# A transformer block with a mixture of experts: in SyncE's order, the loads of k directly behind their store

## The reference

```python
mod = (_silu(L0_c) @ L0_wmod).reshape(B, 6, 1, -1)            # sa, ca, ga, sb, cb, gb
h = _layernorm(x) * (1 + ca) + sa
x = x + ga * attention(h)                                      # 16 heads of 16 features, softmax
h = _layernorm(x) * (1 + cb) + sb
x = x + gb * experts(h)
# experts: 2 shared and 16 routed, 256 -> 128 -> 256 with gelu;
# probs = softmax(h @ router.T); the top 4 of 16 are kept as gates, the others are 0
# act = gelu(up_r) * gate;  routed = sum over experts of act @ down
```

## Time and profile before

| | |
|---|---|
| median of 3 runs | 997.27 us (994.63 to 997.33) |
| the profiled execution | 992.75 us, span 991.0 us |
| TensorE busy (matmuls) | 875.2 us, 88% |
| VectorE busy | 673.8 us, 68% |
| ScalarE busy | 614.9 us, 62% |
| GpSimd busy | 387.3 us, 39% |
| DMA, mean rate | 79 GB/s |
| granted TensorE clock, mean over the span | 0.951 |

### The profile page before, as it was taken

The page is one execution under the profiler, slowest core; times in us unless marked ns, Lnnn a source line. Parts: engine busy times, 40 slices in busy tenths (PEclk is TensorE's granted clock), DMA queues, the critical chain, the costliest instruction groups (busy, mean ns, idle before and its releaser), DMA issues.

```text
span 991.0 us, 15808 instructions
## 1 busy us (share of the span) xinstructions
PE 875.2 (88%) x5928; PEld 424.8 (43%) x5928; DVE 673.8 (68%) x1315; ACT 614.9 (62%) x1033; POOL 387.3 (39%) x325
## 2 busy tenths in 40 slices
PE   5478876889989898999989998999989998998897
PEld 3222123224544454444544454444544454455564
DVE  6686676467678777678678777777767778834332
ACT  3246444575767576876777576767578667773443
POOL 4423023122442534344433444344425233454445
PEclk9758789799999999999999999999999999999999
DMA  6804600371032611371133411271135310320230
GB/s 242 171 0 97 107 1 11 55 167 59 2 93 75 140 48 54 55 177 70 44 55 135 76 48 64 46 197 49 55 54 129 97 44 1 115 96 18 81 118 22
DMA packets 50413, 78.37 MB, mean 79 GB/s; under 512 B 8216, under 2 KB 44568, under 8 KB 46240
## 3 DMA queue, kind: packets, MB, share of 16 engines
q1 hardware_dynamic: 50336, 77.36, 29.9%
HBM read 64.31 MB, written 12.89 MB: 78 GB/s over the span
## 4 chain that ended last, share of the span: by engine, by line
PE 48%; DVE 15%; DMA 11%; ACT 10%; issue 6%; POOL 5%; SPq 4%; POOLq 0%; ACTq 0%; DVEq 0%
PE down_bank L889 13%; PE scalar_bank L758 11%; DMA k_aug<-k_parts 8%; PE vector_bank L821 7%; PE vector_bank L803 6%; PE vector_bank L758 4%; PE scalar_bank L803 4%; DVE q_aug L720 4%; DVE gelu L702 3%; ACT f_ring L535 3%; DVE neg_max L715 3%; POOL z_lo L475 3%; ACT probs L558 3%; DVE rows L600 3%; SPq L408 2%
## 5 line engine op out<-in xcount | busy, mean ns | idle before, releaser
L715 DVE TENSOR_REDUCE neg_max<-vector_bank 128x1 f16<-128x512 f32 x512 | 325.5, 686 | 105.6 <-PE vector_bank L803 104.3
L558 ACT ACTIVATE probs<-scalar_bank 128x512 f32<-128x512 f32 x512 | 277.0, 600 | 188.4 <-PE scalar_bank L803 178.7
L517 POOL TENSOR_TENSOR act_lo<-gelu,act_hi 128x512 f16<-128x512 f32 x144 | 185.7, 1312 | 171.9 <-ACT act_hi L549 162.4
L702 DVE TENSOR_TENSOR gelu<-gelu,gates 128x512 f32<-128x512 f32 x128 | 117.3, 929 | 86.5 <-ACT gelu L583 85.9
L803 PE MATMUL vector_bank<-k_aug,q_aug 64*128 64x512 f16 x512 | 130.1, 414 | 44.5 <-DMA k_aug<-k_parts 28.9
L889 PE MATMUL down_bank<-down_hi,act_hi 128*128 128x256 f16 x576 | 159.1, 276 | 2.1 <-POOL act_lo L517 1.7
L889 PE MATMUL down_bank<-down_hi,act_lo 128*128 128x256 f16 x576 | 157.7, 274 | 0.0
L889 PE MATMUL down_bank<-down_lo,act_hi 128*128 128x256 f16 x576 | 157.7, 274 | 0.0
L803 PE MATMUL scalar_bank<-q_aug,k_aug 64*128 64x512 f16 x512 | 119.4, 400 | 20.3 <-DVE q_aug L720 9.0
L549 ACT ACTIVATE act_hi<-gelu 128x512 f16<-128x512 f32 x128 | 80.4, 628 | 78.9 <-DVE gelu L702 73.4
L821 PE MATMUL vector_bank<-probs,v_aug 128*32 128x512 f32 x1024 | 124.1, 615 | 0.2 <-ACT probs L558 0.2
(11 more groups left out here) (120 smaller groups left out, 1086.1 us busy)
## 6 DMA issues: line engine op xcount, KB each, us to landing
gates<-gates_by_expert SPq DMA_DIRECT2D x32, 1024.0 KB, 4.8
q_aug<-q_parts SPq DMA_DIRECT2D x48, 128.0 KB, 4.7
k_aug<-k_parts SPq DMA_DIRECT2D x48, 128.0 KB, 9.5
x_pre<-in_x SPq DMA_DIRECT2D x8, 512.0 KB, 6.0
x_post<-in_x SPq DMA_DIRECT2D x8, 512.0 KB, 3.8
out<-x_post SPq DMA_DIRECT2D x8, 512.0 KB, 10.0
gates<-in_w_up SPq DMA_DIRECT2D x4, 576.0 KB, 11.0
gates<-in_w_down SPq DMA_DIRECT2D x4, 576.0 KB, 5.7
```

What stands on the lines that cost most here:

```text
L517: pool.tensor_tensor(act[1][:, c, :], gelu[:, n % NGELU, :], act[0][:, c, :], ALU.subtract).then_inc(s_elo, 1)
L558: scalar.activation(probs[:, n % U, :], src[:], ACT.Exp, scale=SCALE).then_inc(taken[kind], 1)
L702: dve.tensor_tensor(g, g, gates[:, (n - NSH) % 8, :], ALU.mult).then_inc(s_gated, 1)
L715: dve.tensor_reduce(neg_max[:, (u // 2) % TT, at:at + 1], src[:], AX.X, ALU.max, negate=True).then_inc(done, 1)
```

## The change

Two numbers in the table: the items that load k go from places 10 and 11 of their slot to place 6. That is behind ("qk_out", 3), which stands at place 5, and in front of "gates_out" at place 7, "gates_in" 0 at place 8, x_pre and mod_pre at place 9 and "gates_in" 1 at place 9.

```diff
           ("qk_out", 0, -4, 16), ("qk_out", 1, -3, 4), ("qk_in", 0, -3, 5), ("qk_in", 1, -3, 6), ("no_max", 0, -3, 7),
-          ("qk_out", 2, -2, 0), ("qk_out", 3, -2, 5), ("qk_in", 2, -2, 10), ("qk_in", 3, -2, 11),
+          ("qk_out", 2, -2, 0), ("qk_out", 3, -2, 5), ("qk_in", 2, -2, 6), ("qk_in", 3, -2, 6),
           ("gates_out", 0, 6, 7), ("gates_in", 0, 6, 8), ("gates_in", 1, 6, 9), ("gates_in", 2, 7, 18), ("gates_in", 3, 8, 18),
```

## The result

The changed kernel takes 1003.38 us in the median of 22 runs, the kernel before 995.53 us in 22 runs beside them. The ratio is 1.0070, 95% interval 1.0052 to 1.0087: slower, by 5 to 9 us. A second series gave 1.0081 (1.0055 to 1.0107). The profiled execution has a span of 996.9 us against 991.0.

What follows compares the result with a forecast made beforehand. It took TensorE's waits for late k loads, 12.9 us, as the cap on the gain; exchanged for gates waits, the batches summed to +3.8 or +2.0, taken as +2.5 on the 997.27 median: 999.8 us, range 989 to 1008.

Steps and rivals of the forecast that it cites:

- rival A: TensorE: k's stall goes, a stall of the same size behind the gates comes; 996 to 1004 us, chance 0.58.
- Steps 1 to 3: From k's store to TensorE: k loads 8.0 us, first product at 13.3, first early exponential 5.2 later, then 0.6.
- Step 4: TensorE's exponential matmuls, six batches: k stalls exchanged for waits behind the gates; sum +3.8 or +2.0, taken as +2.5 us.
- Step 5: Slack elsewhere: ScalarE's idle 3.46 us used up, x_pre, x_post and gates 1 in time; a failure costs 1 to 2 us a batch.
- C: VectorE's first multiplication in six groups: gates become the longer wait, +11.5 us, 1009 us; chance 0.17.
- B: Gates' store slips between the k loads, gates 2.5 us earlier in each of six batches; 986 us, chance 0.22.
- The estimate by the Trainium skill: Gates load of 1 MB: 6.15 us instead of 4.7, 1.45 longer each, result 8.7 us slower; set aside for the row.

## Why the prediction was right or wrong

It was right in its mechanism, the exchange of one wait for another, in its direction and in its range. Its size was low: +2.5 us forecast, 7.0 measured (5.2 to 8.7). 1003.38 lies at the upper end of rival A's own range (996 to 1004), and the clock, which carried part of it there, was no part of A.

Steps 1 to 3, *the terms*, against the pattern of the first profile, in us after k's store has landed (536.54). k loads landed: forecast 8.0, measured 8.0. The gates' store behind them: 8.4, measured 8.2. Gates 0: 4.7, measured 4.5. First product: 13.3, measured 12.7. From it to the first early exponential: 5.2, measured 5.24. To TensorE's matmul: 0.6, measured 0.65. The whole, 19.1, measured 18.6. That the small store lands only behind the k loads, read off batch 0's two small stores, is so at all six batches of this profile (0.2 to 0.3 us behind the last load), and moving this one store in front showed what it was worth. What the step did not have is where TensorE stops first: between 200 and 775 us it waits 7.3 us for VectorE's copy, ahead of the matmul that the forecast named, and only 4.5 us more than before for the exponentials. The pause ended where the forecast said.

Step 4, *the exchange*: batches 3 to 6 were forecast at -0.3, +0.4, +0.25 and +1.2, measured -0.2, -0.2, -0.2 and +0.6. For batch 7 the terms gave +2.7, and the profile has about 2.5 without the fall. But +2.5 for the whole was taken between the sum with that term at 2.7 (+3.8) and with it at 0.9 (+2.0), in case its slow store was an accident, and the store is slow in every profile. By the full term batches 3 to 7 were forecast at +4.3, and the profile has 2.5 of exchange there: that this equals the +2.5 is luck, two errors that cancel. Batch 2 is not read: its place lies where the clock changes all the time from the start on, in every kernel.

What the forecast lacked besides was not a term of the sum. It took every pause at its length. But pauses come with falls of the granted clock, more often the longer they are: the falls at batches 3 to 7 cost some 1.6 us in the first profile of the changed kernel and 8 to 9 in the second, and the run with k alone late had one without any delay of the gates. The profile before had the signs only in what it did not show, as none of its five pauses of 1.4 to 2.7 us (batches 3 to 7) had one behind it; a second profile of the same kernel had two. How the 7 us are shared in the mean over the runs stays open. By the first pair of profiles the exchange at batches 3 to 7 is 2.5, which would leave 4 to 5 to the clock. By the mean clocks of the second series (0.9444 and 0.9472) the clock is worth 2 to 3 us, an estimate, and some 5 would be left to the exchange, twice the forecast. The two don't agree, batch 2 and the stretch behind the last transposes (0.8 and 1.0 us in the first pair) are in neither reading, and no run here decides it.

Step 5, *the covers*, held: ScalarE's idle 3.46 us behind its first exponentials are gone, VectorE waits 4.6 us for gates 0 in the pattern, and no engine waited for x_pre or gates 1. GpSimd did wait for x_post, three times and 1.9 us in all between 200 and 775 us, which it had not before; no other engine is seen waiting on that. Rival A is what happened, at the upper end, with part of C's size. B did not happen: its advantage had to be made by moving the store, and was then worth 10 us against the kernel before. The estimate by the Trainium skill (DMA: Bandwidth & Descriptors, Bandwidth), 8.7 us more for a longer gates load, would have made it +11.2, above the measured 5.2 to 8.7. The load took 4.5 us in the pattern, 4.4 to 5.0 at the six batches, so the row was the right price.

## What to carry to other kernels

Where a small store lands only behind the loads that were issued before it, as here, move only as much ahead as the deadline needs, and look at what is now behind it and when that is due, at small transfers first. Here the 32 KB store stands at the head of a chain (store, 1 MB load, three engines) and cost 18 us by its place alone; the kernel with it in front beats both others. When two waits trade places at equal length the sum is not zero by itself: compare the pauses that TensorE is left with, as longer ones came with falls of its clock here. And a term that looks like an accident in one profile is worth a second profile, or full price.

## What the runs showed of the hardware

- Pauses of TensorE that sum to 2.9 us and more at one place, in a stretch where it is otherwise nearly always busy, came with a fall to half speed for 3.4 or 6.8 us in 10 of 10 cases, pauses of 1.4 to 2.8 us in 9 of 33, differently from run to run of one kernel, and shorter ones in none of 22.
- A 32 KB store issued behind six loads of 128 KB landed 4.9 to 5.7 us after its issue, 0.2 to 0.3 behind the last load (six batches of the changed kernel's first profile). Issued behind two stores of 128 KB in the kernel before, it took 1.6 to 1.7 us at five batches and 3.1 at batch 7, where the store ahead of it was slow.
- 512 KB put in front of that store delayed the first product by 1.4 to 2.7 us, 1.8 in the mean of five batches.
